# Row sums of the exponents from a column of ones in the values instead of ScalarE's accumulator

## The reference

```python
Q = jnp.einsum('bsh,hd->bsd', inputs, Wq) + bq
K = Q
V = Q
scores = jnp.einsum('bqh,bkh->bqk', Q, K) * scale
probs = jax.nn.softmax(scores, axis=-1)
out = jnp.einsum('bqk,bkh->bqh', probs, V)
...
x = x + ga * _L0_attn_ref(h, L0_attn_Wq, L0_attn_bq)
```

## Time and profile before

| | us |
|---|---|
| median of three runs | 352.49 |
| lowest and highest | 351.85 and 352.88 |
| the profiled execution | 352.24 |
| its span, first to last instruction | 350.5 |

### The profile page before, as it was taken

The page is one execution under the profiler, slowest core; times in us unless marked ns, Lnnn a source line. Parts: engine busy times, 40 slices in busy tenths (PEclk is TensorE's granted clock), DMA queues, the critical chain, the costliest instruction groups (busy, mean ns, idle before and its releaser), DMA issues.

```text
span 350.5 us, 8421 instructions
## 1 busy us (share of the span) xinstructions
PE 325.7 (93%) x2580; PEld 300.1 (86%) x2580; DVE 277.5 (79%) x1115; ACT 222.6 (63%) x476; POOL 191.5 (55%) x224
## 2 busy tenths in 40 slices
PE   3899999999999999999989898899999999999960
PEld 3587888889888988898878798899999999999960
DVE  4479898898889888988997886899887677778730
ACT  2588987798779877987775586654445444334310
POOL 4018456645664566446624546777666556565661
PEclk9999999999999999999999999999999999999995
DMA  3294135528763858753636613564999554354300
GB/s 114 81 291 112 34 65 119 145 104 101 150 125 102 111 131 210 212 147 118 110 80 238 233 47 79 188 209 135 298 278 283 164 176 126 113 145 121 93 21 4
DMA packets 34349, 49.21 MB, mean 140 GB/s; under 512 B 4304, under 2 KB 25971, under 8 KB 34304
## 3 DMA queue, kind: packets, MB, share of 16 engines
q1 hardware_dynamic: 27328, 31.66, 38.9%
q0 software_dynamic: 6368, 16.92, 13.0%
q10 hardware_dynamic: 608, 0.08, 0.1%
HBM read 28.15 MB, written 20.96 MB: 140 GB/s over the span
## 4 chain that ended last, share of the span: by engine, by line
PE 69%; DVE 13%; ACT 6%; issue 5%; DMA 2%; DVEq 1%; SPq 1%; POOL 1%; POOLq 0%; ACTq 0%
PE mixed L633 14%; PE mixed L533 12%; PE flipped L520 6%; PE side L483 4%; PE scores L510 3%; PE scores L508 3%; PE scores L509 3%; PE side L553 3%; PE scores L617 2%; PE scores L618 2%; PE side L465 2%; PE scores L616 2%; PE side L545 2%; PE flipped L616 2%; PE flipped L618 2%
## 5 line engine op out<-in xcount | busy, mean ns | idle before, releaser
L1426 POOL DMA_INDIRECT sorted_rows<-payload,slots x64 | 63.8, 996 | 79.5 <-DVE slots L1064 64.5
L1453 POOL DMA_INDIRECT out_dram<-y_out,tokens x71 | 73.8, 1039 | 43.5 <-DVE y_out L1125 27.9
L633 PE MATMUL mixed<-down_slot,hidden 128*128 128x128 f32 x568 | 70.2, 276 | 2.5 <-ACT hidden L819 2.5
L633 PEld LDWEIGHTS mixed<-down_slot,hidden 128*128 128x128 f32 x568 | 66.5, 192 | 3.0 <-ACT hidden L819 3.0
L533 PE MATMUL mixed<-v_sb,probs_t 128*128 128x128 f32 x512 | 69.0, 278 | 0.0
L762 ACT ACTIVATE probs<-scores,row_max 128x512 f32<-128x512 f32 x64 | 43.9, 687 | 34.7 <-DVE row_max L957 33.2
L533 PEld LDWEIGHTS mixed<-v_sb,probs_t 128*128 128x128 f32 x512 | 62.2, 192 | 0.2
L957 DVE TENSOR_REDUCE row_max<-scores 128x1 f32<-128x512 f32 x64 | 44.0, 688 | 19.0 <-PE scores L510 18.9
L804 ACT ACTIVATE f_hi<-side 128x256 fp32r<-128x256 f32 (+1 forms) x39 | 14.2, 365 | 42.7 <-PE side L595 38.5
L520 PE MATMUL flipped<-ident,probs 128*128 128x128 f32 x256 | 39.1, 275 | 0.6 <-ACT probs L762 0.5
L770 ACT ACTIVATE probs_t<-flipped 128x512 f32<-128x512 f32 x64 | 37.8, 593 | 0.0
(11 more groups left out here) (190 smaller groups left out, 769.0 us busy)
## 6 DMA issues: line engine op xcount, KB each, us to landing
rows<-sorted_rows SPq DMA_DIRECT2D x32, 388.0 KB, 3.8
x_tile<-in_L_attn_inputs_dram SPq DMA_DIRECT2D x16, 256.0 KB, 3.2
payload<-stored_gates SPq DMA_DIRECT2D x16, 256.0 KB, 9.6
sorted_rows<-pad_rows SPq DMA_DIRECT2D x9, 388.0 KB, 4.6
w_parts<-in_L_ffn_W_dram SPq DMA_DIRECT2D x1, 2048.0 KB, 10.2
rows<-sorted_rows SPq DMA_DIRECT2D x7, 194.0 KB, 2.8
out_dram<-y_out,tokens POOLq DMA_INDIRECT x71
sorted_rows<-payload,slots POOLq DMA_INDIRECT x64, 5.0
```

Of the source, the lines that this page charges most:

```text
L633: last = nc.tensor.matmul(mixed[t % 2][:, u * H:(u + 1) * H], hidden[:, t % 2, f, u * P:(u + 1) * P], down_slot[:, t % 3, f, :], start=(f ...
L1426: nc.gpsimd.indirect_dma_start(rows_dram, bass.IndirectOffsetOnAxis(ap=slots[:, c:c + 1], axis=0), payload[:, b.q, j, :], None).then_inc(s ...
L1453: nc.gpsimd.indirect_dma_start(out_rows, bass.IndirectOffsetOnAxis(ap=tokens[:, t % RING, u:u + 1], axis=0), y_out[:, t % RING, u, :], Non ...
```

## The change

The values get a 129th column that GpSimd fills with ones once. `mix` multiplies it along, so that column 128 of `mixed` holds the row's sum of exponents. ScalarE's exponent no longer writes a sum, and `den` is gone. `invert_den` and its two calls are gone. Instead `residual` first takes the reciprocal of column 128 of its own block, straight from PSUM, then waits for it, then does what it did. In batch 0 `mix` also waits for the ones.

```diff
-        v_sb = sb("v_sb", [P, 2, J, H])
+        v_sb = sb("v_sb", [P, 2, J, H + 1])
         row_max = sb("row_max", [P, 2 * J])
-        den = sb("den", [P, 2 * J])
...
+                if b.n == 0:
+                    pe.wait_ge(s_ones, 1)
...
-                    last = nc.tensor.matmul(mixed[j % 2][:, 0:H], probs_t[:, j % 2, k * P:(k + 1) * P],
+                    last = nc.tensor.matmul(mixed[j % 2][:, 0:H + 1], probs_t[:, j % 2, k * P:(k + 1) * P],
...
-                nc.scalar.activation(probs[:, j % 2, :], scores[j % 2][:], ACT.Exp, bias=row_max[:, c:c + 1],
-                                     accum_out=den[:, c:c + 1]).then_inc(exp_done, 1)
+                nc.scalar.activation(probs[:, j % 2, :], scores[j % 2][:], ACT.Exp, bias=row_max[:, c:c + 1]
+                                     ).then_inc(exp_done, 1)
...
-                nc.vector.tensor_tensor(v_sb[:, b.p, :, :], side[1][:].rearrange("p (j h) -> p j h", j=J),
+                nc.vector.tensor_tensor(v_sb[:, b.p, :, 0:H], side[1][:].rearrange("p (j h) -> p j h", j=J),
...
-            def invert_den(b, pair):
-                if not real(b):
-                    return
-                dve.wait_ge(exp_done, J * b.n + 2 * pair + 2)
-                c = b.p * J + 2 * pair
-                nc.vector.reciprocal(den_inv[:, c:c + 2], den[:, c:c + 2]).then_inc(den_ready, 1)
-
...
-                dve.wait_ge(den_ready, 2 * b.n + j // 2 + 1)
                 dve.wait_ge(attn_done, J * b.n + j + 1)
                 c = b.p * J + j
+                nc.vector.reciprocal(den_inv[:, c:c + 1], mixed[j % 2][:, H:H + 1]).then_inc(den_ready, 1)
+                dve.wait_ge(den_ready, J * b.n + j + 1)
...
-                invert_den(now, 0)
...
-                invert_den(now, 1)
...
             nc.gpsimd.memset(payload[:, :, :, ROW_ID:ROW], 0.0).then_inc(s_pool, 1)
+            nc.gpsimd.memset(v_sb[:, :, :, H:H + 1], 1.0).then_inc(s_ones, 1)
             pool.wait_ge(s_pool, 4)
```

More of the change, by code:

```diff
@@ L223, in adaln_block @@
         s_pad0 = sem("s_pad0")
+        s_ones = sem("s_ones")
         x_loaded = [sem(f"x_loaded{n}") for n in range(X_TILES)]
```

## The result

The changed kernel is slower: 354.17 us (median of six, 353.97 to 354.72) beside 352.46 (351.66 to 352.94) for the kernel before, ratio 1.0050 [1.0036, 1.0064], so +1.7 us. Forecast: +3.3 and 355.8, range 353.4 to 357.2. Direction and range held, the size was nearly twice too large.

A forecast was written before the change was run, and what follows sets the result against it. TensorE bounds the repeating slots, VectorE and ScalarE the late ones. -0.10 + 0.05 + 0.19 + 1.44 + 0.21 + 0.61 + 0.21 + 0.73 = 3.34 us; on 352.49 that gives 355.8 us, range 353.4 to 357.2.

The forecast's parts named there:

- What bounds, and where it would hurt: TensorE busy throughout k = 3 to 12; one residual between VectorE's last score wait and place makes place 0.20 us later.
- The price of a pair: VectorE, reciprocal plus dependent residual: 0.20 us from start to start, bounds 0.11 and 0.25; removed reciprocals give back nothing.
- The cover: Hand-over from place to flip_xn2's load in repeating slots: 0.055 us spare, so place 0.20 later loses TensorE 0.145.
- The late slots: k = 13, 14 and 15, reciprocals on VectorE's chain: losses of 0.61, 0.21 and 0.73 us.
- The opening: One ScalarE accumulator read saved at the start, where the first block's flip waits for its exponents: 0.10 us gained.
- ScalarE, the column, the rest: Reads hidden in repeating slots; 129th column at most 0.44 us on TensorE's path; memset of ones and its wait nothing.
- The signs named: Period 11.91 us; load waiting for place; residual 0.20 after reciprocal; about 0.37 before find_max(now, 3); k = 13 longer by 0.6.
- B: Repeating slots: a shorter hand-over lets the cover hold, only columns cost there; 1.9 us in all, 354.4; chance 0.15.
- C: VectorE: removed reciprocals give back 0.11 us each; 1.7 us in all, 354.2; chance 0.12.
- D: TensorE's mixes: the odd width costs a tenth of every instruction, 5.6 us; 361; chance 0.03.
- F: ScalarE holds the slots at the stage's edge, so dropped reads gain 1.44 us; 351.3, faster; chance 0.04.
- E: Late slots absorb the delay as well as the repeating ones; 0.8 us, 353.3, no measurable change; chance 0.06.

## Why the prediction was right in direction and too large

**What bounds, and where it would hurt: right.** In k = 9 VectorE's waiting for scores fell from 1.17 us to less than 0.5, so it had room for the work; it still lost, since one of the four reciprocals lies behind the last wait. Moving that one, and then all, took the loss in the profiled slots away in two steps, 0.8 and 1.3 us. The medians show the sum of the two (1.7 down to 0.4) but not the first step (1.7 down to 1.5); the changed kernel's profiled execution was its longest.

**The price of a pair: right by itself, too large on the stretch.** 0.20 was taken, 0.19 measured, from PSUM as from SBUF. The 0.02 for PSUM wasn't there (157 for 152 ns); it had been read in the earlier trace rows from an addition and a multiplication with another operand, not from two additions. The lower bound of 0.11 was no bound: with all moved two instructions start 0.08 apart (131.94 and 132.02). On the stretch the price became 0.15, through two small terms I hadn't: a `residual` without it starts 0.13 after the instruction ahead of it, with it 0.11 + 0.19, so +0.17; and the removed pair reciprocal gave back 0.02 (L1025 follows L1020 by 0.21, L1029 followed L1024 by 0.23).

**The cover: the step that was read wrong.** "The cover is 0.055 us" was read at the weight load: release at 132.20, load at 132.26. But a load isn't the work. In the earlier trace rows it ran 0.11 ahead of its matmul, which stood behind L465's four. With a late release it runs 0.03 ahead, and the matmul is 0.15 behind `place`. Counted at the matmul the cover is 132.37 - 132.09 - 0.15 = 0.13. What the forecast also lacked is the price of the late release, 0.04 behind the matmul, so that the cover is worth not quite 0.09 net. Together: 0.15 - 0.13 + 0.04 = 0.06 per slot, measured 0.07, for which the forecast had 0.16. Of the 0.09 too much, 0.05 is the price on the stretch, 0.03 the cover and 0.01 the column, which adds nothing to the 7.11 of a late release. Nine slots are 0.8 of the 1.2 us by which the sum was too large. So two terms were mis-sized here, and the larger share is the reciprocal's; the cover is the one that was read at the wrong instruction. k = 12 failed in the same way: its matmul stood 0.23 behind `place`, so 0.09 of cover where I had none; +0.11 instead of +0.21.

**The late slots: right.** k = 13 and 15 cost 0.59 and 0.77 for 0.61 and 0.73; there is nothing to cover them. k = 14 had 0.17 for 0.21, all of it on the stretch (5.48 for 5.31).

**The opening: mis-sized.** -0.26 by the reads instead of -0.10 (the table's -0.29 holds a first maximum that starts 0.03 earlier as well). The early cover held: L891 ends at 29.34 + 0.81 = 30.15 with the second of GpSimd's subtractions (27.60 + 2 x 1.25 = 30.10), and k = 1 lost nothing to its two residuals (with the reciprocals alone the opening is 21.57 for 21.56).

**ScalarE, the column, the rest.** No gain from the reads in the repeating slots (11.75 without them): right. The column costs half of the 0.44 us, about 0.2 where TensorE isn't released late; the mixes' mean is 277 for 278 ns.

**The signs named.** The period is 11.82, not 11.91, and so missed. The others came: the load 0.12 behind `place` up to k = 14, the residual 0.19 after its reciprocal, 0.36 before `find_max(now, 3)`, the mixes within 2 ns, k = 13 longer by 0.59.

**The rivals.** B had the cover hold because the hand-over were shorter than 0.11. It is 0.12 at the load in k = 2 to 14, so its reason falls, though part of its effect came another way. C, that removed reciprocals give back 0.11 each, falls: the first gave 0.02, the second nothing (L983 followed `residual(now, 1)` by 0.37 us, L979 now by 0.38). D and F fell to runs of their own. E falls: the late slots absorbed nothing.

**What stays open.** With the reciprocals alone the median rose by 2.9, with the whole change by 1.7. The opening (0.27) and the slots (0.10) account for 0.4 of the 1.2 between them. The rest isn't explained; the medians stand on four and six runs, taken at different times.

## What to carry to other kernels

An engine's idle time pays for new work only where the work stands ahead of the wait; what stands between the engine's last wait and the instruction that others wait for is paid in full, less the cover at that one hand-over. Measure that cover at the instruction that does the work (the matmul), not at its prefetch: a weight load that starts late can still be in time. Then ask what the late start costs behind it. Put an instruction whose result is needed at once into the shadow of another dependence, a few instructions early; here that alone turned +1.7 us into +0.4 with the same work.

## What the runs showed of the hardware that I had not expected

- A weight load of 128x128 ran 0.11 us ahead of its matmul when TensorE was busy and 0.03 ahead when it was released late: 0.08 us of a late release is absorbed. The late start has a price behind it: 0.04 us to the next third maximum, 0.03 of it within the four flips.
- Reading one element per partition from PSUM costs a reciprocal 5 ns (157 for 152 ns), and the dependent instruction starts no later (0.19 us in both).
- A 129th column (rows of 516 bytes) costs TensorE 0.01 to 0.02 us per 32 instructions, and nothing that shows behind a late release (7.11 us to the next third maximum with and without it).
- The same program took 352.4, 367.4 and 371.3 us on different chips, with holds of ScalarE and VectorE of up to 4.7 us that the profile puts down to "remote".
